# Token identifiers loaded by halves of the text, each half to all 128 partitions, in a one-core language tower kernel

## The reference, cut to what matters

```python
amps = emb[x]                                    # 64 values for each token
onehot = one_hot(x, 64).transpose(0, 2, 1)
h = gelu(conv1d(onehot, w1, b1, pad=3))          # 7 taps, 64 -> 128 channels
h = gelu(conv1d(h, w2, b2, pad=2))               # 5 taps, 128 -> 64
ctx = sigmoid(conv1d(h, w3, b3, pad=1))
lp = locality_shapes[x]                          # 4 values for each token
center = linspace(0, 1, 128) + lp[..., 0] * 0.05
z = (positions[:, None, :] - center[..., None]) / (abs(lp[..., 1]) * scale_width + 1e-5)
# for four widths: exp(-z*z/2) * cos(phase + 2*pi*z), weighted and summed; phase = pi * lp[..., 3]
field = einsum('bsp,bsd->bpd', basis_total, amps * ctx)
```

## Time and profile before

| what | us |
|---|---|
| median of three runs | 112.61 |
| the three runs | 111.65, 112.61, 113.19 |
| the profiled execution, its own time | 111.52 |
| its span, first to last instruction | 109.6 |
| TensorE busy | 100.5 (92%) |
| VectorE busy | 90.0 (82%) |
| ScalarE busy | 70.8 (65%) |

### The profile page before, as it was taken

One profiled execution on the slowest core, in us unless ns is written; L12 is line 12 of the kernel. 1 busy time (PEld: TensorE's weight loads), 2 busy tenths in 40 slices (PEclk: granted clock), 3 DMA queues, 4 the chain that ended last, 5 costly groups with the idle time before them and its releaser, 6 DMA issues.

```text
span 109.6 us, 2018 instructions
## 1 busy us (share of the span) xinstructions
PE 100.5 (92%) x723; PEld 64.3 (59%) x723; DVE 90.0 (82%) x230; ACT 70.8 (65%) x126; POOL 51.0 (47%) x101
## 2 busy tenths in 40 slices
PE   5979999999999978869899999999999799999970
PEld 2356785364434576347567477876696476776640
DVE  0359999999999949999999599678999956199892
ACT  4604599999999999999869438454758513551000
POOL 7798998899980007205509426256005000000670
PEclk9999999999999999999999999999999999999999
DMA  3999700000000100000000000000000000000044
GB/s 91 269 233 408 283 0 0 3 0 0 6 0 4 5 0 0 0 0 6 0 0 0 0 6 0 0 0 0 0 0 9 0 0 0 0 0 0 0 96 96
DMA packets 4313, 4.15 MB, mean 38 GB/s; under 512 B 3280, under 2 KB 3536, under 8 KB 4176
## 3 DMA queue, kind: packets, MB, share of 16 engines
q1 hardware_dynamic: 4160, 3.92, 12.5%
q10 hardware_dynamic: 144, 0.12, 0.4%
HBM read 3.50 MB, written 0.52 MB: 37 GB/s over the span
## 4 chain that ended last, share of the span: by engine, by line
PE 42%; ACT 38%; DVE 8%; DMA 4%; issue 4%; POOL 2%; ACTq 0%; DVEq 0%
PE pair L1080 14%; ACT wave L476 8%; PE bank L1042 7%; ACT bell L466 7%; ACT bell L470 5%; ACT L425 5%; DMA ids<-x 4%; DVE pair L819 3%; PE hid_pair L1053 3%; PE pair L951 3%; ACT angle L514 3%; PE pair L921 2%; ACT h L460 2%; PE hid_pair L1063 2%; ACT dist L455 2%
## 5 line engine op out<-in xcount | busy, mean ns | idle before, releaser
L379 POOL TENSOR_SCALAR var_eps<-mean_var 128x4 f32<-128x4 f32 x8 | 3.7, 458 | 33.0 <-DVE mean_var L747 33.0
L819 DVE COPY_PREDICATED pair<-later,pair 128x256 f32<-128x256 int32 (+3 forms) x30 | 12.3, 409 | 5.3 <-PE pair L1080 4.6
L921 PE MATMUL pair<-warm 128*128 128x512 bf16 x53 | 13.3, 380 | 0.0
L732 DVE SCALAR_TENSOR_TENSOR bell<-bell,scale_w,wave 128x512 f32<-128x512 f32 x16 | 10.8, 743 | 0.0
L1080 PE MATMUL pair<-wd_high,H_high 128*128 128x512 f32 x32 | 10.8, 418 | 0.0
L921 PE MATMUL hid_pair<-warm 128*128 128x512 bf16 x30 | 9.0, 455 | 1.3 <-POOL warm L298 1.3
L1080 PE MATMUL pair<-wd_low,H_high 128*128 128x512 f32 x32 | 10.0, 394 | 0.0
L395 POOL TENSOR_TENSOR angle<-picked,prob 128x256 f32<-128x256 f32 x3 | 1.8, 613 | 17.2 <-DVE prob L843 17.2
L521 ACT ACTIVATE bell<-hid_pair,sm 128x512 f32<-128x512 f32 x8 | 5.0, 680 | 7.2 <-PE hid_pair L1053 7.2
L675 DVE TENSOR_TENSOR wave<-dist,inv_width 128x2048 f32<-128x2048 f32 x4 | 9.3, 2356 | 0.0
L965 PE MATMUL pair<-h,w_sb 128*64 128x512 f32 x40 | 9.1, 597 | 0.0
(11 more groups left out here) (166 smaller groups left out, 226.1 us busy)
## 6 DMA issues: line engine op xcount, KB each, us to landing
ids<-x SPq DMA_DIRECT2D x2, 512.0 KB, 5.7
posb<-positions SPq DMA_DIRECT2D x1, 768.0 KB, 8.1
wd_sb<-wd SPq DMA_DIRECT2D x1, 512.0 KB, 9.1
out<-angle SPq DMA_DIRECT2D x3, 128.0 KB, 2.0
st_sb<-state SPq DMA_DIRECT2D x1, 328.0 KB, 8.3
w_sb<-w SPq DMA_DIRECT2D x1, 256.0 KB, 6.6
posb<-positions SPq DMA_DIRECT2D x1, 256.0 KB, 6.6
w_sb<-w SPq DMA_DIRECT2D x1, 160.0 KB, 8.0
```

The source lines that it names most:

```text
L732: ins = dve.scalar_tensor_tensor(out=bell[:, g, part], in0=bell[:, g, part], scalar=scale_w[:, s:s + 1], in1=wave[:, g, part], op0=ALU.mul ...
L819: return dve.copy_predicated(held[:, :, 0:n, 0, 0:D], repeat(later[:, g, 2 * h + rows.start:2 * h + rows.stop, first:first + n], 3, D), he ...
L921: pe.matmul(bank[free], warm[:, 0:P], warm[:, :], start=True, stop=True)
```

## The change

It has seven edits.

1. Each identifier transfer takes half of the text (1024 places, the second 1023) and writes all 128 partitions. The shift of the upper half is made by the source pattern: its counts are 2 (step 1), 64 (step 0) and n (step 1).
2. Two transfers of 64 identifiers of 4 bytes each, issued by ScalarE behind the small table, fill in the end columns (semaphore `ends`).
3. VectorE compares by halves: onehot_b, onehot, then the same of the second half, then the two edge columns.
4. The place negated is made by ScalarE early on (neg_place), so that VectorE gives the negative centres in one instruction; the centres go. The low part of w1 moves behind them. ScalarE makes all the distances, those of group 0 too, and its copy of w1's high part moves ahead of the copy of the shapes, the tanh behind the distances of group 0.
5. VectorE's angles are split in two functions (phases and wrap), and phases(3) moves ahead of moments(0, 0).
6. TensorE: 10 fillers at the start, shapes of the first half, 5 fillers, shapes of the second half, 4 fillers, conv 1. The first embeddings move from before conv 1 to behind the taps, with 8 fillers in place of 10.
7. ScalarE's upright_out(0) moves ahead of a table load (load_gelu).

```diff
-            for half in range(2):
-                sp.dma_start(ids[half * V:half * V + V, 1 - half:1 - half + NB * P],
-                             repeat(row, 0, V)).then_inc(ld[f"x{half}"], 16)
+            for part in range(2):
+                first = part * (NB * P // 2)
+                n = NB * P // 2 - part
+                both = bass.AP(tensor=row.tensor, offset=row.offset + first, ap=[[1, 2], [0, V], [1, n]])
+                sp.dma_start(ids[:, 1 + first:1 + first + n], both).then_inc(ld[f"x{part}"], 16)
...
             act.dma_start(sm[:, :], small).then_inc(ld["small"], 16)
+            row = x.rearrange("b t -> (b t)")
+            act.dma_start(ids[0:V, NB * P:NB * P + 1], repeat(row[NB * P - 1:], 0, V)).then_inc(ld["ends"], 16)
+            act.dma_start(ids[V:, 0:1], repeat(row[0:1], 0, V)).then_inc(ld["ends"], 16)
...
+            act.activation(neg_place[:, :], col("place"), ACT.Copy, scale=-1.0).then_inc(s_place, 1)
...
             load_gelu()
+            act.wait_ge(ld["w1"], 16)
+            act.copy(w1p[0][:], w1_sb[:]).then_inc(s_w1_part, 1)
             act.wait_ge(s_shapes_mm, 1)
             act.copy(shapes[:, :, :].rearrange("p b c -> p (b c)"), bank[6][:, 0:NB * NL]).then_inc(s_shapes, 1)
             act.wait_ge(s_shapes, 1)
-            act.activation(amp_tanh[:, :], shapes[:, :, 2], ACT.Tanh, scale=0.5).then_inc(s_amp_tanh, 1)
-            act.wait_ge(ld["w1"], 16)
-            act.copy(w1p[0][:], w1_sb[:]).then_inc(s_w1_part, 1)
-            act.wait_ge(s_center, 1)
-            act.activation(neg_center[:, :], center[:, :], ACT.Copy, scale=-1.0).then_inc(s_negc, 1)
             act.wait_ge(s_negc, 1)
...
+            distances(0)
+            act.activation(amp_tanh[:, :], shapes[:, :, 2], ACT.Tanh, scale=0.5).then_inc(s_amp_tanh, 1)
             distances(1)
+            distances(2)
             conv1_out(0)
-            distances(2)
             conv1_out(1)
...
             field_out(0)
+            upright_out(0)
             load_gelu()
-            upright_out(0)
...
+            for part in range(2):
+                n = slice(part * NB // 2, (part + 1) * NB // 2)
+                dve.wait_ge(ld[f"x{part}"], 16)
+                if part == 0:
+                    dve.wait_ge(s_pad, 2)
+                else:
+                    dve.wait_ge(ld["ends"], 32)
+                dve.tensor_scalar(onehot_b[:, n, :], from_first[0:V, n], value[0:V], None,
+                                  ALU.is_equal).then_inc(s_onehot, 1)
+                dve.tensor_scalar(onehot[:, n, 3:2 + P], from_first[:, n, 0:P - 1], value, None, ALU.is_equal)
...
+            dve.wait_ge(s_shapes, 1)
+            dve.wait_ge(s_place, 1)
+            lp = [shapes[:, :, k] for k in range(NL)]
+            dve.tensor_scalar(neg_center[:, :], lp[0], -0.05, neg_place[:, 0:1], ALU.mult,
+                              ALU.add).then_inc(s_negc, 1)
...
-            dve.wait_ge(ld["pos0"], 16)
-            dve.wait_ge(s_center, 1)
-            link(dve.tensor_tensor(dist[:, 0:GB, :], posb[:, 0:GB, :], repeat(center[:, 0:GB], 2, P), ALU.subtract))
...
-            keep_warm(14, 7)
+            keep_warm(10, 7)
...
-            for b in range(NB):
-                mm = look_up(bank[6][:, b * NL:(b + 1) * NL], b, slice(D, D + NL))
+            for part in range(2):
+                pe.wait_ge(s_onehot, part + 1)
+                for b in range(part * NB // 2, (part + 1) * NB // 2):
+                    mm = look_up(bank[6][:, b * NL:(b + 1) * NL], b, slice(D, D + NL))
+                if part == 0:
+                    keep_warm(5, 7)
...
-            keep_warm(3, 7)
-            embeddings(0)
-            keep_warm(3, 7)
-            pe.wait_ge(s_onehot, 2)
+            keep_warm(4, 7)
+            pe.wait_ge(s_onehot, 3)
             conv1((0, 1))
...
-            keep_warm(10, 6)
+            keep_warm(8, 6)
+            embeddings(0)
             context(0)
```

More of the change, by code:

```diff
@@ L131, in tower @@
         amps = sb("amps", [P, NB, D])
-        center = sb("center", [P, NB])
+        neg_place = sb("neg_place", [P, 1])
         absw = sb("absw", [P, NB])
@@ L206, in tower @@
         H_high, H_low = (sb(f"H_{n}", [P, 2, KH, T], F32R) for n in ("high", "low"))
-        ld = {n: sem(f"ld_{n}") for n in ("x0", "x1", "pos0", "pos", "small", "w1", "w2", "state", "wd", "bd", "bias")}
+        ld = {n: sem(f"ld_{n}") for n in ("x0", "x1", "ends", "pos0", "pos", "small", "w1", "w2", "state", "wd", "bd", "bias")}
         stored = sem("stored")
@@ L216, in tower @@
         s_w1_part = sem("s_w1_part")
-        s_center, s_warm = sem("s_center"), sem("s_warm")
+        s_place, s_warm = sem("s_place"), sem("s_warm")
         s_copied = [sem("s_copied0"), sem("s_copied1")]
@@ L443, in _ @@
             act.wait_ge(s_shapes, 1)
-            act.activation(amp_tanh[:, :], shapes[:, :, 2], ACT.Tanh, scale=0.5).then_inc(s_amp_tanh, 1)
-            act.wait_ge(ld["w1"], 16)
-            act.copy(w1p[0][:], w1_sb[:]).then_inc(s_w1_part, 1)
-            act.wait_ge(s_center, 1)
-            act.activation(neg_center[:, :], center[:, :], ACT.Copy, scale=-1.0).then_inc(s_negc, 1)
             act.wait_ge(s_negc, 1)
             def distances(g):
-                act.wait_ge(ld["pos"], 16)
+                act.wait_ge(ld["pos" if g else "pos0"], 16)
                 for b in range(g * GB, (g + 1) * GB):
@@ L636, in _ @@
             dve.tensor_tensor(scale_w[:, :], col("weights"), col("weights"), ALU.mult)
-            dve.wait_ge(ld["x0"], 16)
             from_first, from_zero = (ids[:, k:k + NB * P].rearrange("p (b t) -> p b t", b=NB) for k in (1, 0))
             value = col("value")
[L641 to L645, removed]
+            for part in range(2):
[8 more added lines that the diff above has]
+                dve.tensor_scalar(onehot[:, n, 3:2 + P], from_first[:, n, 0:P - 1], value, None, ALU.is_equal)
             dve.tensor_scalar(onehot[0:V, :, 2 + P:3 + P], from_first[0:V, :, P - 1:P], value[0:V], None,
@@ L649, in _ @@
                               ALU.is_equal).then_inc(s_onehot, 1)
-            dve.wait_ge(s_w1_part, 1)
[L651 to L656, removed]
+            dve.wait_ge(s_shapes, 1)
[3 more added lines that the diff above has]
+                              ALU.add).then_inc(s_negc, 1)
+            dve.scalar_tensor_tensor(out=absw[:, :], in0=lp[1], scalar=-1.0, in1=lp[1], op0=ALU.mult, op1=ALU.max)
+            dve.wait_ge(s_w1_part, 1)
+            link(dve.tensor_tensor(w1p[1][:], w1_sb[:], w1p[0][:].bitcast(F32), ALU.subtract))
+            dve.sem_inc(s_w1_part, 1)
             for s in range(NS):
@@ L664, in _ @@
             link(dve.tensor_scalar(phase_tmp[:, 1, :], phase_tmp[:, 0, :], -ROUND, -0.75, ALU.add, ALU.add))
-            dve.scalar_tensor_tensor(out=phase[:, :], in0=lp[3], scalar=0.5, in1=phase_tmp[:, 1, :],
-                                     op0=ALU.mult, op1=ALU.subtract)
-            dve.wait_ge(ld["pos0"], 16)
-            dve.wait_ge(s_center, 1)
-            link(dve.tensor_tensor(dist[:, 0:GB, :], posb[:, 0:GB, :], repeat(center[:, 0:GB], 2, P), ALU.subtract))
+            link(dve.scalar_tensor_tensor(out=phase[:, :], in0=lp[3], scalar=0.5, in1=phase_tmp[:, 1, :],
+                                          op0=ALU.mult, op1=ALU.subtract))
             def z(g):
-                if g:
-                    dve.wait_ge(s_rest[g], 1)
+                dve.wait_ge(s_rest[g], 1)
                 dve.tensor_tensor(
@@ L679, in z, with phases @@
                     ALU.mult).then_inc(s_z[g], 1)
-            def turns(g):
+            def phases(g):
                 dve.wait_ge(s_z[g], 1)
@@ L689, in turns, with wrap @@
                 link(ins)
+            def wrap(g):
                 dve.tensor_scalar(angle[:, g, :], angle[:, g, :], TURN_MASK, None,
@@ L853, in _ @@
             z(1)
-            turns(0)
-            turns(1)
-            z(2)
-            turns(2)
+            phases(0)
+            wrap(0)
+            phases(1)
+            wrap(1)
+            z(2)
+            phases(2)
+            wrap(2)
             gates(0)
@@ L861, in _ @@
             z(3)
+            phases(3)
             moments(0, 0)
-            turns(3)
+            wrap(3)
             normalise(0, 0)
@@ L923, in _ @@
             pe.wait_ge(s_warm, 1)
-            keep_warm(14, 7)
+            keep_warm(10, 7)
             pe.wait_ge(s_emb_split, 1)
-            pe.wait_ge(s_onehot, 1)
             def look_up(where, b, cols):
```

## The result

The changed kernel takes 132.63 us (median of four runs, 132.41 to 132.84), the kernel before 112.13 in the same comparison: a ratio of 1.1815, with a 95% interval of 1.1712 to 1.1917. 129.4 was predicted, and the time lies in the likeliest case's own range of 126 to 134.

The account below looks back on a forecast made before the run. The chain of waits from the identifiers to conv 2's gelu, then a full ScalarE, was taken to bound the kernel. Losses of 16.7 + 0.1 = 16.8 us on 111.5 gave 128.3, with 1.1 for the median 129.4; range 110.5 to 134.

Parts of the forecast that it names:

- the likeliest case: Identifier transfers on two engines, the loss as summed: 129.4 us, own range 126 to 134, chance 0.65.
- How the transfer is dealt out: Identifier transfers: shares are cut along the outermost count of 2, so two engines carry what sixteen did.
- The landings: Identifier transfers: the first lands at 13.6 us, the second at 23.9, 16.0 later than 7.9.
- The term of 10.3 us a transfer: Each identifier transfer: 512 KB on two engines at 50.8 GB/s; 9.8 or 12.0 us with other base rates.
- w1 behind the identifiers: Load of w1, queued on the same two engines: lands 0.65 us after the second identifier transfer, at 24.6 us.
- The clock: TensorE before conv 1: its clock falls back while idle, costing 1.4 us, between bounds of 0 and 1.9.
- ScalarE's readiness: Before conv 2's gelu: ScalarE's work ends near 39.3 us, just ready for 39.7, so TensorE decides.
- Edit 7: Around 39 us of before: ScalarE's copy waits 0.5 us, VectorE gets it about 1 us sooner; loss of 0.1 taken.
- The sum: Whole kernel: 16.7 us at conv 2's gelu plus 0.1 around 39 us, 16.8 us of loss.
- Rival A: Identifier transfers on all sixteen engines at 406 GB/s, landing at 4.6 and 5.9 us: 111.0 us, chance 0.23.
- My reading of 213 GB/s as the price of 64 partitions: Identifier transfers before: half the rate because partitions 0 to 63 reach half of the DMA ports.
- the sentence that the trace agrees with the page: Identifier transfers: the trace's 213 against 399 to 430 GB/s agrees with the skill's half of the DMA ports.

Follow-up runs that it names:

- rows4: The changed kernel with the text laid out in 4 rows on the host, so the source's outermost count is 4: 125.69 us in one run.
- rows16: The changed kernel with the text in 16 host rows, 8 of them one place later, so the source's outermost count is 16: 114.46 us.
- edit1_alone: The kernel before with only the new identifier transfers and end columns, compares whole and waiting for both: 135.89 us, ratio 1.2113.
- kept_warm: The changed kernel with TensorE's fillers lengthened, 54 for 10 at the start and 55 for 5 between the shapes' halves: 130.89 us, ratio 1.1736.
- the last two runs: The changed kernel with 16 host rows holding the end columns and 16, 5 and 1 fillers: 111.92 us; the same with edit 7 undone: 111.00 us.
- tight_upright_back: The changed kernel with 16 host rows holding the end columns, 16, 5 and 1 fillers, and edit 7 undone: 111.00 us, ratio 0.9958.
- rows16_warm: rows16 with TensorE's fillers lengthened, 21 for 10 and 10 for 5: 114.90 us, ratio 1.0252.

## Why the prediction was right, and where it wasn't

**How the transfer is dealt out: right.** Two engines for a count of 2, four for 4, sixteen for 16, with nothing else changed between rows4 and rows16. The Trainium skill (DMA: Bandwidth & Descriptors, section Why a DMA increments its semaphore by 16 and not by 1) gives this rule, and also says that the issuing engine adds the missing updates at once; the semaphores agree, with fourteen at 1.84 us and two at 13.93 and 14.23.

**The landings: the first right, the second mis-sized.** 13.6 and 23.9 were summed, 14.2 and 27.0 came. The term of 10.3 us a transfer was too low for the second, which took 12.8 (12.3 in edit1_alone, 11.6 in kept_warm). Alone, from 22 to 26 us, the two engines move 51 to 52 GB/s, as summed. Between 14 and 22 us the other loads run on the fourteen engines beside them, with a share over all sixteen of 0.97 and 0.89, and the pieces of 4092 bytes take 201 ns in the mean, the first transfer's 167. By time they take 162 ns before 14 us, 229 to 264 from 16 to 22, and 161 to 164 behind. I had counted the loads behind the identifiers as waiting for them; their shares on the idle engines run beside them, and I take them to slow them. That is argued from the times, not tested.

**w1 behind the identifiers: right.** 0.65 us behind the second landing were predicted, the copy of w1 starts 0.65 after it (27.71 against 27.06). The positions land at 28.34 and 30.25, 0.65 and 1.9 us behind w1 and each other, as summed. They cost nothing beyond, as predicted: the distances didn't wait for them.

**The clock: right in kind, too small.** 1.4 us were taken between bounds of 0 and 1.9; the rows of the change against kept_warm give 2.1. It fell in the first wait and stayed at 0.50 through the second and into conv 1 (0.63 from 30 to 34 us, 1.00 from 34).

**ScalarE's readiness: right.** TensorE decided the start of conv 2's gelu; ScalarE waited 0.54 us for it.

**Edit 7: wrong by 0.4 to 0.8.** I took a loss of 0.1 between -0.5 and 0.5. ScalarE was the full engine there, and no gain from VectorE's sooner start is seen, so all of the 0.53 us counts: the profile shows 0.5 to 0.6 behind conv 2's gelu, and the last two runs 0.7 to 0.9.

**The sum: near in part by luck.** From profile to profile the loss is 21.3 us, and 16.8 were summed. Of the 4.5 between, 3.1 are the second landing, 0.9 lie between it and conv 2's gelu (0.7 of them the clock), and 0.4 behind that. The end figures are only 3.2 apart, because I added 1.1 us for a median above its profiled execution: before, the median of the comparison stands 0.6 above it, and the changed kernel's 0.2 below.

**Rival A: mispriced.** For sixteen engines I gave 111.0 to the change as written. rows16, the nearest to it, took 112.4 to 115.1. Two steps failed. The rate was taken from other loads with 128 partitions (406 GB/s), and the identifiers got 238: landings of 6.8 and 9.0 for 4.6 and 5.9. And with edit 6's fewer fillers the clock fell in the profiled run, which I had priced only for the long waits of two engines. The most that this form gave is 0.4% (tight_upright_back), with the fillers fitted and edit 7 undone.

**What stays open.** Why do identifier pieces move at 213 to 260 GB/s on sixteen engines, before and in rows16, when positions move at 400? Not the number of partitions alone, the offset of one place, the source's address or the moment at which it runs. What is left is the way in which the rows fall to the engines: in rows16 the source has 16 rows of 8 copies, so each engine may write 8 partitions in a row, while for the positions both sides have 128. The Trainium skill (SBUF — State Buffer, section Door 1: The DMA port swizzle) says that partitions 32 apart share a DMA port; by that, engines that work on such rows at the same time would slow each other, in rows4 as well. No run here shows it. The change's two engines, whose halves lie 64 apart, kept 26 GB/s each while they ran alone. A source with 128 rows on the host would tell, and wasn't tried.

My reading of 213 GB/s as the price of 64 partitions isn't disproved by this, but 128 partitions alone didn't mend it, and the sentence that the trace agrees with the page claimed more than the rows held.

## What to carry to other kernels

Read the outermost count of both sides of a transfer before anything else: in these runs 2, 4 and 16 gave as many DMA engines, and one pattern of 2 turned the 2.3 us between the two landings into 12.8. Count the semaphore's updates in the trace to see how many engines there were. When a load moves, fit the fillers to the new landings in both directions, and don't move a copy that waits for another engine ahead of a table load that hid the wait.

## What the runs showed that I had not expected

SyncE stalls behind transfers with two engines: the issue of w1 took 8.66 us (0.58 before), and the next five 1.0 to 2.0 each, so that the loads behind are not even handed out. With four engines (rows4) w1's took 0.47, and only two later ones 1.5 and 1.9.

Four engines were hardly faster than two: the first landing at 12.92 against 14.23 us.

In rows16 TensorE had a pause from 5.1 to 7.7 us, with the first fillers as the only work before it, and the granted clock then read 0.50 (the 1.2 GHz level) from 8 us on. In kept_warm and rows16_warm, with no such pause, it reads 1.00 through conv 1.

At the start the granted clock reads 1.00 although the fillers are 0.43 us apart, the pace of the lower level. The moment at which they quicken isn't the same in every execution: 4.3 us in rows16 and tight_upright_back, 5.1 in the kernel before, 7.1 in rows16_warm. The same number of fillers thus ends at different times, and a mean granted clock of 1.00 doesn't say that the clock was high from the start.
